# Spectral convolution in pairs of filters: short Toeplitz pieces share a matmul, with two sets of split rows

## What is computed

```python
Vf = jnp.fft.rfft(phi, n=n, axis=0)
Uf_p = jnp.fft.rfft(u, n=n, axis=1)
Uf_m = jnp.fft.rfft(u * sgn3, n=n, axis=1)
U_plus = jnp.fft.irfft(Vf[None, :, :, None] * Uf_p[:, :, None, :], n=n, axis=1)[:, :sl]
U_minus = jnp.fft.irfft(Vf[None, :, :, None] * Uf_m[:, :, None, :], n=n, axis=1)[:, :sl]
...
out = jnp.einsum('btkd,k,kde->bte', U_plus, s, Mpp)
out = out + jnp.einsum('btkd,k,kde->bte', U_minus, s, Mpm)
```

## Time and profile before

| | |
|---|---|
| runs | 850.28, 850.33, 851.41 us; median 850.33 |
| profiled execution | 850.71 us |
| its span, first to last instruction | 848.9 us |
| TensorE (PE) busy | 665.4 us, 78% |
| VectorE (DVE) busy | 624.4 us, 74% |
| ScalarE (ACT) busy | 349.7 us, 41% |
| GpSimd (POOL) busy | 424.1 us, 50% |
| convolution matmuls, line 1619 | 768, 127.8 us busy by the page |

### The profile page before, as it was taken

One profiled execution on the slowest core, in us unless ns is written; L12 is line 12 of the kernel. 1 busy time (PEld: TensorE's weight loads), 2 busy tenths in 40 slices (PEclk: granted clock), 3 DMA queues, 4 the chain that ended last, 5 costly groups with the idle time before them and its releaser, 6 DMA issues. The chain is left out here.

```text
span 848.9 us, 7033 instructions
## 1 busy us (share of the span) xinstructions
PE 665.4 (78%) x2460; PEld 352.4 (42%) x2460; DVE 624.4 (74%) x603; ACT 349.7 (41%) x379; POOL 424.1 (50%) x231
## 2 busy tenths in 40 slices
PE   2788788788797877888777777382867599999997
PEld 2442223222222322223222222161434488888886
DVE  6289999999999899999999569647671424443342
ACT  3485365474653736537335035142003223332231
POOL 5039989899899899999977300000231000000000
PEclk9989999999999999999999888798776589999999
DMA  5044444544444445445454160201900000000000
GB/s 161 3 149 149 156 154 142 178 167 153 150 151 145 153 152 185 140 140 182 152 175 169 53 272 0 107 1 48 349 0 0 1 1 1 0 0 0 0 0 25
DMA packets 27226, 88.33 MB, mean 104 GB/s; under 512 B 3636, under 2 KB 4374, under 8 KB 26462
## 3 DMA queue, kind: packets, MB, share of 16 engines
q1 hardware_dynamic: 27200, 88.01, 29.7%
HBM read 86.87 MB, written 1.13 MB: 104 GB/s over the span
## 5 line engine op out<-in xcount | busy, mean ns | idle before, releaser
L576 POOL TENSOR_TENSOR area<-area 128x1024 f32<-128x1024 f32 x127 | 299.4, 2373 | 75.8 <-DVE area L1088 54.9
L1088 DVE TENSOR_TENSOR_SCAN area<-area,ps 128x1024 f32<-128x1024 f32 x128 | 289.4, 2274 | 0.0
L1370 PE MATMUL ps<-area,cst 128*128 128x512 f32 x512 | 256.1, 624 | 1.4 <-POOL area L576 1.1
L755 ACT ACTIVATE area<-area,floors,par_sb 128x1024 f32<-128x1024 f32 x128 | 158.1, 1239 | 177.5 <-DVE area L1088 175.2
L1081 DVE TENSOR_TENSOR ps<-ps,area 128x1024 f32<-128x1024 f32 x128 | 154.2, 1211 | 7.8 <-PE ps L1349 7.2
L1370 PEld LDWEIGHTS ps<-area,cst 128*128 128x128 f32 x512 | 88.5, 191 | 108.1 <-issue 100.6
L1619 PE MATMUL ps<-stack 128*128 128x512 f32 (+3 forms) x768 | 127.8, 326 | 0.4 <-DVE stack L1271 0.4
L1619 PEld LDWEIGHTS ps<-stack 128*128 128x128 f32 x768 | 117.0, 192 | 11.9 <-issue 2.6
L1349 PE MATMUL ps<-stack,sel 32*128 32x512 f32 x256 | 63.7, 495 | 71.4 <-DVE area L1088 67.2
L437 DVE COPY area<-ps 64x1024 f32<-64x1024 f32 x32 | 39.3, 1227 | 85.7 <-PE ps L1619 85.7
L1349 PEld LDWEIGHTS ps<-stack,sel 32*128 32x128 f32 x256 | 23.7, 182 | 162.8 <-DVE area L1088 139.3
(11 more groups left out here) (285 smaller groups left out, 651.0 us busy)
## 6 DMA issues: line engine op xcount, KB each, us to landing
area<-c_rows SPq DMA_DIRECT2D x128, 512.0 KB, 3.8
area<-phi_scaled SPq DMA_DIRECT2D x1, 4104.0 KB, 25.3
area<-in_m_phi_dram SPq DMA_DIRECT2D x4, 1024.0 KB, 8.6
area<-phi_scaled SPq DMA_DIRECT2D x1, 4096.0 KB, 14.9
area<-in_q_t_dram SPq DMA_DIRECT2D x1, 1024.0 KB, 14.1
area<-in_dft_dram SPq DMA_DIRECT2D x1, 784.0 KB
area<-in_m_u_dram SPq DMA_DIRECT2D x1, 768.0 KB, 6.1
area<-in_conv_w_dram SPq DMA_DIRECT2D x1, 576.0 KB, 6.0
```

What stands on the lines that cost most here:

```text
L576: pool.tensor_tensor(scan_order(prod[:, u % PRODS, :], k), lines(state[:, u % STATES, :], k), lines(c_sb[:, u % COPIES, :], k), MUL).then_ ...
L755: act.activation(decay[:, u % DECAYS, :], delta[:, n % 2, :], ACT.Exp, bias=floors[:, k, i:i + 1], scale=par_sb[:, k, i:i + 1]).then_inc(s ...
L1088: dve.tensor_tensor_scan(state[:, u % STATES, :], decay[:, u % DECAYS, :], drive_pair(u), 0.0, MUL, ADD).then_inc(sig("scanned"), 1)
L1370: mm = pe.matmul(ps[:, 6 + h, :], con("center"), half(prod[:, u % PRODS, :], h), start=False, stop=(u % (UNITS // 2) == UNITS // 2 - 1), s ...
```

## The change

Filters are convolved in pairs. A call `convolve(p, parity, g)` handles one `(s, t)` for both filters of pair `p`, with g = 2s + t. The two banks it writes are now two time halves `y` of 256 outputs, and inside a bank the two filters `a` lie side by side (`p (a n) -> p a n`). A matmul streams the same piece of both filters' rows, as two runs that lie a fixed distance apart in `toep_hl`. A piece that crosses the middle is cut in two, one for each bank. For q = 0 to 3 the column counts become 512 and 512; 256 and 512; 512; 256: six matmuls for each `i`, 18 for a call, 72 for a pair, 576 in all. The products and the columns streamed are the same.

The split rows have two sets, each with both filters of a pair. The set for the next pair is written while this one is convolved. The tokens' split `xn_hl` moves to the selector's space, `u_t` to that of `z_gate`; `area` shrinks and `stack` grows. The copies out of PSUM are as many and as large as before, but each takes both filters' signals of one `(s, t)` and writes them in four runs of 256. They wait for both mixes of the pair before. The two mixes of a pair stand together, behind the first call of the next pair; the last two stand together behind the autoregressive matmuls.

```diff
-        xn_hl = spare[:, 0:2 * L].rearrange("p (s n) -> p s n", s=2)
-        toep_hl = spare[:, 2 * L:2 * L + 4 * TOE].rearrange("p (a s n) -> p a s n", a=2, s=2)
+        b_rows = spare[0:64, B * PAD + FRONT:B * PAD + FRONT + STACKED].rearrange("p (s n) -> p s n", s=2)
+
+        xn_hl = sel[:].rearrange("p i m -> p (i m)").rearrange("p (s n) -> p s n", s=2)
+        toep_hl = [t.rearrange("p (a s n) -> p a s n", a=2, s=2) for t in (
+            spare[:, 0:4 * TOE], spare[:, 4 * TOE:8 * TOE])]
...
-        def filtered(engine, k, a, s):
-
-            wait(engine, sig("convolved"), 2 * k + s + 1)
-            if s == 0 and (not isinstance(k, int) or k >= 2):
-                engine.wait_ge(sig("mixed"), k - 1)
+        def filtered(engine, p, g):
+
+            s, t = divmod(g, 2)
+            wait(engine, sig("convolved"), 4 * p + g + 1)
+            if g == 0:
+                wait(engine, sig("mixed"), 2 * p)
             b = 0 if engine is nc.scalar else 1
-            dst, src = filt[64 * s:64 * s + 64, a, b, :], banks(2 + 2 * s)[64 * b:64 * b + 64]
+            dst = filt[64 * s:64 * s + 64, :, b, t * HALF:(t + 1) * HALF].rearrange("p a (y n) -> p y a n", y=2)
+            src = ps[64 * b:64 * b + 64, 2 + 2 * (g % 2):4 + 2 * (g % 2), :].rearrange("p y (a n) -> p y a n", a=2)
...
-            def pair_of(k0, more):
-                for a in range(2):
-                    for s in range(2):
-                        filtered(engine, k0 + a, a, s)
-                    if more:
-                        split_rows(k0 + 2 + a, a)
-            pair_of(0, True)
-            with engine.Fori(1, KF // 2 - 1) as pair:
-                pair_of(2 * pair, True)
-            pair_of(KF - 2, False)
+            def pair(p, parity, more):
+                for g in range(4):
+                    filtered(engine, p, g)
+                    if more and g < 2:
+                        split_rows(2 * p + 2 + g, 1 - parity, g)
+
+            pair(0, 0, True)
+            with engine.Fori(0, KF // 4 - 1) as twice:
+                pair(2 * twice + 1, 1, True)
+                pair(2 * twice + 2, 0, True)
+            pair(KF // 2 - 1, 1, False)
...
-            def toep_high(k, a):
-
-                if not isinstance(k, int) or k >= 2:
-                    act.wait_ge(sig("convolved"), 2 * k - 2)
-                act.activation(toep_hl[:, a, 0:1, :], toep[:, bass.ds(k, 1), :], ACT.Copy).then_inc(sig("toep_high"), 1)
+            def toep_high(k, parity, a):
+
+                if not isinstance(k, int) or k >= 4:
+                    act.wait_ge(sig("convolved"), 2 * (k - a) - 4)
+                act.activation(toep_hl[parity][:, a, 0:1, :], toep[:, bass.ds(k, 1), :],
+                               ACT.Copy).then_inc(sig("toep_high"), 1)
...
-            def convolve(k, a, s):
-
-
-                if s == 0:
-                    pe.wait_ge(sig("toep_low"), k + 1)
-                if not isinstance(k, int) or k >= 1:
-                    for b in range(B):
-                        pe.wait_ge(sig(f"filtered_{b}"), 2 * k + s - 1)
-                for t in range(2):
-                    for q in range(4):
-                        n, first, j = HALF - P * q, (0 if s == 0 else HALF + t), 2 * q + (t ^ s)
-                        for i, (x_part, row_part) in enumerate(((0, 0), (0, 1), (1, 0))):
-                            mm = pe.matmul(ps[:, 2 + 2 * s + t, P * q:HALF], xn_hl[:, x_part, j * P:(j + 1) * P],
-                                           toep_hl[:, a, row_part, first:first + n],
-                                           start=(q + i == 0), stop=(q == 3 and i == 2))
+            def convolve(p, parity, g):
+
+
+                s, t = divmod(g, 2)
+                if g == 0:
+                    pe.wait_ge(sig("toep_low"), 2 * p + 2)
+                for b in range(B):
+                    wait(pe, sig(f"filtered_{b}"), 4 * p + g - 1)
+                first = 0 if s == 0 else HALF + t
+                for q in range(4):
+                    j = 2 * q + (t ^ s)
+                    for i, (x_part, row_part) in enumerate(((0, 0), (0, 1), (1, 0))):
+                        for y in range(q // 2, 2):
+                            at = max(q, 2 * y)
+                            n, row = P * (2 * y + 2 - at), first + P * (at - q)
+                            mm = pe.matmul(
+                                ps[:, 2 + 2 * (g % 2) + y, :].rearrange(
+                                    "p (a n) -> p a n", a=2)[:, :, P * (at - 2 * y):2 * P],
+                                xn_hl[:, x_part, j * P:(j + 1) * P],
+                                toep_hl[parity][:, :, row_part, row:row + n],
+                                start=(q + i == 0), stop=(q == 2 * y + 1 and i == 2))
                 mm.then_inc(sig("convolved"), 1)
...
-                    pe.wait_ge(sig(f"filtered_{b}"), 2 * k + 2)
+                    pe.wait_ge(sig(f"filtered_{b}"), 2 * (k - a) + 4)
...
-            convolve(0, 0, 0)
-            convolve(0, 0, 1)
+            def pair(p, parity):
+
+                for g in range(4):
+                    convolve(p, parity, g)
+                    if g == 0:
+                        for a in range(2):
+                            mix(2 * p - 2 + a, a, isinstance(p, int) and p == 1 and a == 0)
+
+            for g in range(4):
+                convolve(0, 0, g)
             convolve(1, 1, 0)
             pe.wait_ge(sig("u_t_ready"), 2)
-            mix(0, 0, True)
-            convolve(1, 1, 1)
-            with pe.Fori(1, KF // 2) as pair:
-                convolve(2 * pair, 0, 0)
-                mix(2 * pair - 1, 1)
-                convolve(2 * pair, 0, 1)
-                convolve(2 * pair + 1, 1, 0)
-                mix(2 * pair, 0)
-                convolve(2 * pair + 1, 1, 1)
+            for a in range(2):
+                mix(a, a, a == 0)
+            for g in range(1, 4):
+                convolve(1, 1, g)
+            with pe.Fori(1, KF // 4) as twice:
+                pair(2 * twice, 0)
+                pair(2 * twice + 1, 1)
...
+            mix(KF - 2, 0)
             mix(KF - 1, 1, last=True)
```

More of the change, by code:

```diff
@@ L124, in program @@
         PAD, FRONT, STACKED = 34 * 34, 22 * DI, 2 * HALF
-        stack = sb("stack", [P, B * PAD + FRONT + STACKED], F32R)
+        stack = sb("stack", [P, max(B * PAD + FRONT + STACKED, 8 * TOE)], F32R)
         merge = con("merge").rearrange("p (h r m) -> p h r m", h=2, r=2)
         split = con("split").rearrange("p (r m) -> p r m", r=2)
-        AREA = 36 * L + KF
+        AREA = 36 * L - 640
         DECAYS, STATES, PRODS, COPIES = 4, 4, 3, 3
@@ L156, in program @@
         w_rows = take(ND * 64).rearrange("p (k a m) -> p k a m", k=ND, a=2)
-        assert cut[0] <= 30 * L
-        cut[0] = 30 * L
         spec = take(2 * L).rearrange("p (r n) -> p r n", r=4)
@@ L201, in program @@
         b_exp_sb = take(UN * C)
-        prods = (ln_q[:, 0:512], ln_q[:, 512:L], w_qv_sb, take(512))
+        prods = (ln_q[:, 0:512], ln_q[:, 512:L], w_qv_sb, area[:, later + 3584:later + 4096])
         cut[0] = KF * TOE + 4 * L
@@ L218, in program @@
         cut[0] = tail
-        u_t = take(2 * (HALF + 1)).rearrange("p (t n) -> p t n", t=2)
         fin = ln_c
         z_gate = sb("z_gate", [P, B, L])
+        u_t = z_gate[:].rearrange("p b n -> p (b n)")[:, 0:2 * (HALF + 1)].rearrange("p (t n) -> p t n", t=2)
         w_gate_sb = sb("w_gate_sb", [P, 3, 2, 64])
@@ L239, in program @@
         front_hl = spare[:, B * PAD:B * PAD + FRONT].rearrange("p (s n) -> p s n", s=2)
-        b_rows = spare[0:64, B * PAD + FRONT:].rearrange("p (s n) -> p s n", s=2)
-        xn_hl = spare[:, 0:2 * L].rearrange("p (s n) -> p s n", s=2)
-        toep_hl = spare[:, 2 * L:2 * L + 4 * TOE].rearrange("p (a s n) -> p a s n", a=2, s=2)
+        b_rows = spare[0:64, B * PAD + FRONT:B * PAD + FRONT + STACKED].rearrange("p (s n) -> p s n", s=2)
+        xn_hl = sel[:].rearrange("p i m -> p (i m)").rearrange("p (s n) -> p s n", s=2)
+        toep_hl = [t.rearrange("p (a s n) -> p a s n", a=2, s=2) for t in (
+            spare[:, 0:4 * TOE], spare[:, 4 * TOE:8 * TOE])]
         sig_sb = sb("sig_sb", [2 * KF, 4])
@@ L991, in _ @@
             act.activation(wt_sb, ps[:, 6, 0:P], ACT.Copy).then_inc(reach("w_out_ready"), 1)
-            def toep_high(k, a):
-                if not isinstance(k, int) or k >= 2:
-                    act.wait_ge(sig("convolved"), 2 * k - 2)
-                act.activation(toep_hl[:, a, 0:1, :], toep[:, bass.ds(k, 1), :], ACT.Copy).then_inc(sig("toep_high"), 1)
+            def toep_high(k, parity, a):
[3 more added lines that the diff above has]
+                               ACT.Copy).then_inc(sig("toep_high"), 1)
             act.wait_ge(sig("toep_in"), 32)
             for a in range(2):
-                toep_high(a, a)
+                toep_high(a, 0, a)
             norm_act(act, link, 5)
@@ L1256, in _, with toep_low @@
                     copy_g(dve, l + 1, dve.tensor_copy, ps[:, 7, 0:P])
```

(9 more changed lines are left out.)

## The result

| | before | after |
|---|---|---|
| median | 850.33 us | 839.0 us (5 runs, 838.47 to 839.65) |
| ratio, 95% interval | | 0.9864 (0.9848 to 0.988) |
| profiled execution, span | 850.71, 848.9 | 838.86, 837.1 |

The forecast was 838.2 us in 834.0 to 843.0, 12.1 us less than before. Between the two profiled executions lie 11.85 us, between the medians 11.3.

The account below looks back on a forecast made before the run. TensorE's stream was taken to bound the stage from 681.07 us on. Fewer matmuls 10.8, strided stream -0.4, paired mixes 1.1 + 0.6, copies nothing: 12.1 us off the 850.33 median gave 838.2 us, range 834.0 to 843.0.

Parts of the forecast that it names:

- What bounds the stage: From 681.07 us to the end TensorE's stream sets the time; a microsecond off it is one off the end.
- Part 1: Convolution: 576 matmuls in place of 768, a call 3.49 us where two quarters took 3.83; 10.8 us saved.
- Part 2: Convolution matmuls stream two runs of rows; one gap more costs 0.0007 us each, 0.4 us lost in all.
- sign of being wrong: Convolution: the forecast fails if a 512-column start is over 0.24 us, or TensorE waits for line 436 or 438.
- dear end: Convolution matmuls' second run costs as much as line 1302's fifteen gaps: 5.0 us lost, 842.8 us; chance 0.11.
- cheap one: Convolution matmuls reusing the weights of the one ahead come cheaper: at most 9.4 us gained, 829 us; chance 0.10.
- Part 3: Mixes in twos: 1.1 us from less disturbed convolution, 0.6 us from entering and leaving mixes.
- upper bound of 1.1: Mixes: 8 x 0.14 us if entering and leaving is saved between two in a row; half, 0.6, was taken.
- break: A mix standing inside a convolution costs that convolution 0.14 us more; eight fewer save 1.1 us.
- Part 4: Copies, splits and waits on ACT, DVE and POOL cost nothing, covered by TensorE's calls; first copy's spare 2.3 us.
- rival of the late copy: TensorE's third call waits for the first copy, which waits for two mixes; slower than before; chance 0.02.
- The other rivals: Convolution: strided stream at half speed, 931 us, chance 0.03; or surplus not from the matmuls' number, 848.6 us, 0.02.

## Why the prediction was right

**What bounds the stage** was read rightly: 12.0 us off TensorE's stream were 12.0 us off the end, no engine came forward, and nothing ahead of the stage changed.

**Part 1**, 10.8 us by 192 fewer matmuls, is shown by the count and by the run that leaves the 128-column matmuls out: 0.108 us for each of these, and by its starts 0.232 for 512 contiguous columns and 0.118 for 256, the prices of the sum. The profile after has parts 1 and 2 together, 3.83 - 3.517 = 0.31 us a call and 10.0 in all, where 10.4 was forecast.

**Part 2** took 0.4 us lost for the strided stream. The four undisturbed calls are 3.47, 3.52, 3.54 and 3.54 us, 3.517 on average, where 3.492 was the price with nothing lost: 32 x 0.025 = 0.8 us lost. So the term was too small by half. By the starts, a 512-column matmul takes 0.2335 us on average and one of 256 0.1189, against 0.2318 and 0.1178 contiguous in the run without the short ones. The reason given, one gap more, isn't shown: the calls differ with the address, and one of the four kinds lies under 3.492. The forecast's sign of being wrong, a 512-column start over 0.24, is reached by single starts (the longest is 0.241) but not by the average. The dear end (5.0 us, as at line 1302) and the cheap one (9.4 us gained by reused weights) are both excluded: within a call, the second matmul on the same weights is no faster than the first.

**Part 3** was right in kind. The convolution and the mixes were to give 1.1 and 0.6 us; the mixes gave 1.3 (30.1 to 28.8), over the upper bound of 1.1, since two in a row take 3.60 and not 3.76. The convolution as a whole gave 10.7 (126.7 to 116.0) where 10.8 - 0.4 + 1.1 = 11.5 was forecast. Half of this miss is part 2's. The other half, by estimate, is the break itself: the four calls of a pair take 14.26 us on average, 0.19 over 4 x 3.517, where 0.14 was taken for a break, and eight times 0.05 is 0.4. So the forecast had 0.8 too much for the convolution and 0.7 too little for the mixes. That these cancel is luck: with 0.06 us from the autoregressive matmuls the sum is 12.0 beside 12.1, closer than its terms.

**Part 4**, nothing for copies and splits, holds with a spare of 2.2 us on the first copy, and doubled copies cost 0.2. The rival of the late copy is a true mechanism that this order of the mixes keeps out: with the mixes apart it costs 1.4 us a pair.

**The other rivals** are out: a 512-column matmul takes 0.230 to 0.234 us and not 0.43, and 256 columns written as two runs of 128 take 0.12, as contiguous ones did. The Trainium skill ("PSUM — Partial Sum Buffer", section "Specifications (TRN2)") says that "any non-contiguous AP slows matmuls significantly". For outputs in two runs of 128 this trace disagrees, with the same 0.12 us.

The median came out 0.8 us above the forecast; the profiled execution 0.3 above its 838.6. The runs spread over 1.2 us, so no cause is named for that.

## What to carry to other kernels

When every matmul loads its weights, one of 128 columns costs nearly as much as one of 256 (0.11 against 0.12 us here): below 256 columns count matmuls, not columns, and join short pieces into strided ones of 256 to 512. Two runs of 128 or 256 cost at most 0.002 us a matmul here. Before grouping work, draw the timeline of who releases the buffers: here the grouping is worth 12 us with two sets of rows and both mixes behind the first call, and loses 38 us with one set. And look at the granted clock where TensorE waits: fifteen unneeded matmuls in its gaps were worth 8 us.

## What the runs showed of the hardware

512-column fp32r matmuls start 0.225 to 0.241 us apart, by a pattern that moves with the padding of the streamed rows and whose rule the padding didn't find. From pair 2 on, the calls of the changed kernel and of the one with seven extra matmuls agree in it to 1 ns. A wait of 4.9 us in TensorE's stream cost up to 2.8 us more behind it (a first call of 6.4 us in place of 3.6), where the granted clock had fallen from 2.4 to 1.2 GHz. Filling the gap from 671 to 677 us with matmuls whose result nobody reads kept it at 2.4, and two short ones a round did the same in a stage that is busy for three quarters of the time and yet stood at 0.57.
